# Experts of 24 token tiles computed by gathered rows, with exp buffers of two key tiles

## The reference

```python
qkv = x @ w_qkv; q, k, _ = split(qkv); k2 = own and previous window of 128 keys; v2 = k2
x0 = layernorm(x + (softmax(mask(q @ k2.T / 16)) @ v2) @ w_out + b_out)

q = k = rope(x0); v = x0          # in_proj with bias, 16 heads of width 16
attn = softmax(causal(q @ k.T / 4)) @ v   # over 2048 keys
x1 = layernorm(x0 + attn @ Wo.T + bo) * ln1_w + ln1_b
gates = softmax(x1 @ gate_w.T + gate_b)   # 8 experts
moe = sum over the 2 largest gates g_e: g_e * (x1 @ expert_w[e].T + expert_b[e])
x2 = layernorm(x1 + moe) * ln2_w + ln2_b
out = layernorm(x0 + x2)
```

## Time and profile before

| | us |
|---|---|
| median of 3 runs (1437.79 to 1442.79) | 1440.35 |
| profiled execution, device time | 1441.97 |
| its span from first to last instruction | 1440.2 |
| PE busy | 1388.6 |
| DVE busy | 1088.4 |
| ACT busy | 784.5 |
| POOL busy | 427.2 |
| last `pv` ends, from the span's start | about 1397.6 |

### The profile page before, as it was taken

How to read it: one execution, slowest core, us unless ns; L and a number is a source line. 1 busy time by engine, 2 the same in 40 slices (tenths; PEclk the granted TensorE clock), 3 DMA queues, 4 the chain that set the end, 5 groups by cost and what they waited for, 6 DMA issues and landing times.

```text
span 1440.2 us, 28031 instructions
## 1 busy us (share of the span) xinstructions
PE 1388.6 (96%) x9600; PEld 778.4 (54%) x9600; DVE 1088.4 (76%) x2736; ACT 784.5 (54%) x1707; POOL 427.2 (30%) x707
## 2 busy tenths in 40 slices
PE   8899999999999999999999999999999999999995
PEld 6767655554455545354656655555444355555542
DVE  3765877887797887778645897878778787888745
ACT  3235365555665555665654445554656567655651
POOL 4434522322232131112433543333121110111233
PEclk9999999999999999999999999999999999999997
DMA  3865422231211121121115232222120011111100
GB/s 116 196 175 130 126 57 61 57 80 27 64 47 47 40 59 46 28 57 27 48 54 148 80 90 68 57 58 64 31 60 21 23 26 26 34 32 43 25 23 12
DMA packets 161511, 88.56 MB, mean 61 GB/s; under 512 B 114166, under 2 KB 157998, under 8 KB 161115
## 3 DMA queue, kind: packets, MB, share of 16 engines
q1 hardware_dynamic: 161371, 86.78, 23.1%
HBM read 60.71 MB, written 25.43 MB: 60 GB/s over the span
## 4 chain that ended last, share of the span: by engine, by line
PE 47%; DVE 5%; issue 2%; ACT 2%; POOL 1%; DMA 1%; SPq 1%; POOLq 0%; DVEq 0%; ACTq 0%
PE bank L1533 11%; PE bank L1420 10%; PE bank L1397 8%; PE bank L1369 8%; DVE mxs L1061 2%; PE bank L1490 1%; ACT pbuf L974 1%; PE bank L1509 1%; PE bank L1373 1%; PE bank L1402 1%; PE bank L1519 1%; PE bank L1468 1%; PE bank L1451 1%; PE bank L1476 1%; PE bank L1426 0%
## 5 line engine op out<-in xcount | busy, mean ns | idle before, releaser
L1061 DVE TENSOR_REDUCE mxs<-bank 128x1 f32<-128x512 f32 (+3 forms) x1120 | 708.8, 667 | 145.7 <-PE bank L1369 75.3
L974 ACT ACTIVATE pbuf<-bank 128x512 f32<-128x512 f32 (+1 forms) x1112 | 589.0, 599 | 313.9 <-PE bank L1397 138.6
L1369 PE MATMUL bank<-ks,qs 96*128 96x512 bf16 (+3 forms) x1280 | 423.2, 349 | 5.8 <-DVE mxs L1061 3.5
L1397 PE MATMUL bank<-qs,ks 99*128 99x256 bf16 (+3 forms) x1536 | 421.8, 319 | 5.4 <-DVE mxs L1061 2.1
L1420 PE MATMUL bank<-pbuf,vcur 128*17 128x256 f32 (+3 forms) x3072 | 253.5, 469 | 0.3
L1397 PEld LDWEIGHTS bank<-qs,ks 99*128 99x128 bf16 x1536 | 142.6, 98 | 161.0 <-issue 41.1
L1533 PE MATMUL bank<-ew,x1T 128*128 128x512 f32 x464 | 222.4, 601 | 0.4 <-DVE mxs L1061 0.3
L1369 PEld LDWEIGHTS bank<-ks,qs 96*128 96x128 bf16 x1280 | 123.6, 99 | 128.9 <-issue 40.9
L1420 PEld LDWEIGHTS bank<-pbuf,vcur 128*17 128x17 f32 x3072 | 79.9, 97 | 147.4 <-issue 109.6
L1533 PEld LDWEIGHTS bank<-ew,x1T 128*128 128x128 f32 x464 | 82.0, 190 | 72.4 <-issue 60.8
L954 ACT ACTIVATE etmp<-bank,small 128x256 f32<-128x256 f32 x116 | 48.7, 471 | 80.2 <-PE bank L1533 80.2
(11 more groups left out here) (279 smaller groups left out, 1753.1 us busy)
## 6 DMA issues: line engine op xcount, KB each, us to landing
vcur<-v_scratch SPq DMA_DIRECT2D x92, 136.0 KB, 2.4
parts_scratch<-parts SPq DMA_DIRECT2D x29, 384.0 KB, 3.3
xw<-windows SPq DMA_DIRECT2D x29, 256.0 KB, 2.8
qs<-parts_scratch SPq DMA_DIRECT2D x32, 192.0 KB, 3.7
ks<-parts_scratch SPq DMA_DIRECT2D x28, 192.0 KB, 3.6
qs<-parts_scratch SPq DMA_DIRECT2D x32, 128.0 KB, 3.1
v_scratch<-vst SPq DMA_DIRECT2D x29, 136.0 KB, 2.3
x_scratch<-x SPq DMA_DIRECT2D x29, 128.0 KB, 1.7
```

The lines of the kernel that those rows point to most:

```text
L974: nc.scalar.activation(pbuf[:, u0:u0 + heads, nj * P - cols:nj * P], bk[:, 0:heads * cols].rearrange("p (h t) -> p h t", h=heads), ACT.Exp)\
L1061: v.reduce_max(mxs[:, j * HJ + h:j * HJ + h + heads, c], bk[:, 0:heads * cols].rearrange("p (h t) -> p h t", h=heads), AX_X)\
L1369: last = mm(bk[:, x * cols:(x + 1) * cols].rearrange("p (n t) -> p n t", t=P), qs6[0:KR, pos % QRING, head // HJ, j, head % HJ, :], ks5[0: ...
L1397: last = mm(bk[:, x * cols:(x + 1) * cols].rearrange("p (n t) -> p n t", t=P), ks5[0:KR + NPART, kslot, kb % GT, head, :], qs6[0:KR + NPAR ...
```

## The change

For the first 24 tiles (steps T < `SPARSE`) the dense expert steps are gone. The tiles are taken in three chunks of eight. For each tile x1 is stored in DRAM (`f_st`), as is x1 plus the weighted expert biases, and DVE and PE count which tokens chose which expert (`f_A` to `f_gt`). When a chunk is complete, DVE computes a table (`t_tab`): a place for each of the 2048 token and expert pairs, sorted by expert and padded so that each of 23 blocks of 128 rows has one expert. POOL scatters the tokens' numbers and gates to these places in 16 indirect transfers (`t_sc`), and SP loads the list (`t_id`). For each block SP loads the expert's weights (256 KB, `s_w`, the address read from the table), POOL gathers the rows of x1 (`s_g`), PE transposes (`s_T`) and multiplies by the one expert (`s_e`), ACT copies (`s_Tc`) and scales by the gates (`s_ec`), and SP stores the block (`s_st`). At last each tile's sum is loaded (`b_load`), and two indirect transfers of POOL add the two chosen rows to it (`b_g1`, `b_g2`, into two buffers by turns), behind which the norms run as steps `h_`, which are the `g_` steps on other buffers. The last eight tiles stay dense.

To make room in SBUF, `VRUN` goes from 4 to 2: `pbuf` is half as long, and PE does `pv` in runs of at most two key tiles. The whole order is computed anew, with the new steps' durations and, for the indirect transfers, times until they have landed (`INDIRECT`). The values 1300 and 1900 ns are what the change writes down for one indirect transfer on POOL.

```diff
-VRUN = 4
+VRUN = 2
...
+INDIRECT = {"s_g": 3600, "b_g1": 4000, "b_g2": 5000, "t_sc": 3600}
...
+SPARSE = 24
+CHUNK = 8
+CHUNKS = SPARSE // CHUNK
+BLOCKS = 2 * CHUNK + NE - 1
...
+    add("w_lists", 0, "POOL", 2500)
+    rows["w_lists", 0] = *rows["w_lists", 0][:2], 1.5, rows["w_lists", 0][3]
+    add("w_tri8", 0, "DVE", 100, ("w_lists", 0))
+    add("load_dummy", 0, "SP", 1500, ("w_lists", 0))
...
-        add("f_e0", T, "PE", 1720, ("d_x1Tc", T))
+        if T < SPARSE:
+            c, u = T // CHUNK, T // CHUNK * BLOCKS
...
+            add("f_A", T, "DVE", 100, ("f_ixf", T), ("t_tab", c - 1), ("w_tri8", 0))
+            add("f_A12", T, "DVE", 90, ("f_A", T), ("f_rk", T - 1), ("f_as", T - 1))
+            add("f_rk", T, "PE", 200, ("f_A12", T), ("f_as", T - 1), ("w_lists", 0))
+            add("f_as", T, "DVE", 90, ("f_rk", T), ("t_cnt", c - 1))
+            add("f_Rb", T, "DVE", 90, ("f_rk", T), ("t_tab", c - 1))
+            add("f_gt", T, "DVE", 90, ("f_top", T), ("t_sc", c - 1))
+            add("f_st", T, "SP", 900, ("f_acc0", T))
...
+            add("b_load", T, "SP", 450, ("f_st", T), ("h_aff2", T - 2), ("s_st", u + BLOCKS - 1))
+            add("b_g1", T, "POOL", 1900, ("t_tab", c), ("s_st", u + BLOCKS - 1), ("b_load", T))
+            add("b_g2", T, "POOL", 1900, ("b_g1", T))
+            back = c * CHUNK + CHUNK - 1 + 6 + 1.2 + (2.6 + 0.5 * i if c < CHUNKS - 1 else 1.3 + 0.25 * i)
...
+                add("t_cnt", c, "PE", 150, ("f_as", T))
+                add("t_tab", c, "DVE", 3500, ("t_cnt", c), ("f_Rb", T), ("f_gt", T), ("b_g2", c * CHUNK - 1), ("s_st", c * BLOCKS - 1), ("w_tri8", 0))
+                add("t_sc", c, "POOL", 2 * CHUNK * 1300, ("t_tab", c), ("load_dummy", 0))
+                add("t_id", c, "SP", 2500, ("t_sc", c), ("s_st", c * BLOCKS - 1))
...
+                    add("s_w", u + x, "SP", 900, ("t_tab", c), ("s_e", u + x - 2), ("w_o", 0))
+                    add("s_g", u + x, "POOL", 1300, ("t_id", c), ("f_st", last), ("s_T", u + x - 2))
+                    add("s_T", u + x, "PE", 215, ("s_g", u + x), ("s_Tc", u + x - 1))
+                    add("s_Tc", u + x, "ACT", 300, ("s_T", u + x), ("s_e", u + x - 2))
+                    add("s_e", u + x, "PE", 900, ("s_Tc", u + x), ("s_w", u + x))
+                    add("s_ec", u + x, "ACT", 300, ("s_e", u + x), ("s_st", u + x - 2), *[("h_store", c * CHUNK - 1)] * (x < 2))
+                    add("s_st", u + x, "SP", 900, ("s_ec", u + x))
...
+            add("h_load", T, "SP", 450, ("st0", tile), ("h_store", T - 2), ("s_st", u + BLOCKS - 1))
+            add("h_st", T, "DVE", 330, ("b_g2", T), ("h_norm3", T - 1))
+            add("h_mv", T, "DVE", 100, ("h_st", T))
+            add("h_rstd2", T, "POOL", 950, ("h_mv", T))
+            add("h_xb", T, "POOL", 700, ("h_load", T), ("h_rstd2", T))
+            add("h_norm2", T, "DVE", 370, ("h_mv", T))
+            add("h_aff2", T, "DVE", 370, ("h_norm2", T), ("h_xb", T))
+            add("h_zst", T, "DVE", 330, ("h_aff2", T))
+            add("h_zmv", T, "DVE", 100, ("h_zst", T))
+            add("h_rstd3", T, "POOL", 950, ("h_zmv", T))
+            add("h_norm3", T, "DVE", 320, ("h_rstd3", T))
+            add("h_store", T, "SP", 450, ("h_norm3", T))
...
+        wslot = [lodge(EC * E).rearrange("p (c d) -> p c d", c=EC) for _ in range(2)]
+        xslot, yslot = [lodge(E) for _ in range(2)], [lodge(E) for _ in range(2)]
+        xTslot = [lodge(EC * P).rearrange("p (c t) -> p c t", c=EC) for _ in range(2)]
...
+        accB, x0B = [lodge(E), yslot[0]], [lodge(E), yslot[1]]
...
+                elif name == "t_id":
+                    sp.wait_ge(ids_stored, 16 * 2 * CHUNK * (T + 1))
+                    if T:
+                        for x in range(T * BLOCKS - 2, T * BLOCKS):
+                            sp.wait_ge(xslot_loaded[x % 2], 16 * (x // 2 + 1))
+                    sp.dma_start(ids.rearrange("p (t o) -> p t o", o=2), id_dram[T].rearrange("(t p) o -> p t o", p=P),
+                                 allow_slow_non_contiguous=True).then_inc(ids_loaded, 16)
...
+                elif name == "s_w":
+                    u, t = T, T % BLOCKS
+                    sp.wait_ge(tab_step, TABS * (u // BLOCKS + 1))
+                    if u >= 2:
+                        sp.wait_ge(*fill("s_e", u - 2))
+                    col = sp.value_load(tab_w[0:1, t:t + 1], min_val=0, max_val=(NE - 1) * E)
+                    sp.dma_start(wslot[u % 2], exp_t[:, bass.ds(col, E)].rearrange("(c p) d -> p c d", p=P))\
+                        .then_inc(wslot_loaded[u % 2], 16)
...
+                elif name == "t_sc":
+                    pool.wait_ge(tab_step, TABS * (T + 1))
+                    if T == 0:
+                        pool.wait_ge(ids_loaded, 16 * CHUNKS)
+                    for x in range(2 * CHUNK):
+                        pool.indirect_dma_start(id_dram[T], bass.IndirectOffsetOnAxis(ap=placed[:, x:x + 1], axis=0),
+                                                own[:, x // 2, x % 2, :], None).then_inc(ids_stored, 16)
...
+                elif name == "s_g":
+                    u, t = T, T % BLOCKS
+                    pool.wait_ge(ids_loaded, 16 * (CHUNKS + u // BLOCKS + 1))
+                    pool.wait_ge(x1_stored, 16 * CHUNK * (u // BLOCKS + 1))
+                    if u >= 2:
+                        pool.wait_ge(*fill("s_T", u - 2))
+                    pool.indirect_dma_start(xslot[u % 2], None, x1_dram[u // BLOCKS], bass.IndirectOffsetOnAxis(
+                        ap=ids[:, 2 * t:2 * t + 1], axis=0)).then_inc(xslot_loaded[u % 2], 16)
...
+                elif name in ("b_g1", "b_g2"):
+                    k = int(name[3]) - 1
+                    if k == 0:
+                        pool.wait_ge(tab_step, TABS * (T // CHUNK + 1))
+                        pool.wait_ge(acc_loaded[T % 2], 16 * (T // 2 + 1))
+                        blocks_stored(pool, T)
+                    else:
+                        pool.wait_ge(gathered[T % 2], 32 * (T // 2) + 16)
+                    pool.indirect_dma_start(accB[T % 2], None, ys_dram[T // CHUNK], bass.IndirectOffsetOnAxis(
+                        ap=placed[:, 2 * (T % CHUNK) + k:2 * (T % CHUNK) + k + 1], axis=0), compute_op=ALU.add)\
+                        .then_inc(gathered[T % 2], 16)
...
+                elif name == "s_T":
+                    pe.wait_ge(xslot_loaded[T % 2], 16 * (T // 2 + 1))
+                    for c in range(EC):
+                        last = tr(bk[:, c * P:(c + 1) * P], xslot[T % 2][:, c * P:(c + 1) * P], idf[:, :])
+                    last.then_inc(filled[b], 1)
...
+                elif name == "s_e":
+                    pe.wait_ge(*drain("s_T", T))
+                    pe.wait_ge(wslot_loaded[T % 2], 16 * (T // 2 + 1))
+                    for c in range(EC):
+                        last = mm(bk[:, 0:E], xTslot[T % 2][:, c, :], wslot[T % 2][:, c, :], start=c == 0, stop=c == EC - 1)
+                    last.then_inc(filled[b], 1)
...
+                elif name == "s_ec":
+                    u = T
+                    act.wait_ge(*fill("s_e", u))
+                    if u >= 2:
+                        act.wait_ge(yslot_stored[u % 2], 16 * (u // 2))
+                    if u >= BLOCKS and u % BLOCKS < 2:
+                        act.wait_ge(back_out[1], 16 * (u // BLOCKS * CHUNK // 2))
...
```

423 lines of the change are left out of this document (344 added, 79 removed).

## The result

The changed kernel takes 1423.38 us (median of 4 runs, 1421.59 to 1425.19); the kernel before took 1440.31 beside it (1437.79 to 1442.79). The ratio is 0.9875, with a 95% interval from 0.9861 to 0.9889: 1.25% less, some 18 us. The forecast was 1397.

A forecast was written before the change was run, and what follows sets the result against it. PE's list of work was taken to bound the kernel up to the last pv, with an engine-to-engine tail behind. Work ending at 1323.2, new waits of 20 and a tail of 54 gave 1397 us, range 1364 to 1445.

The forecast's parts named there:

- What bounds the kernel: Whole kernel before: PE's list of work sets the time up to the last pv, then a 42.6 us engine-to-engine tail.
- PE's sum, -65.4: PE's work: dense steps -165.1, blocks +74.5, counting matmuls +5.0, shorter runs +20.2, together -65.4 us.
- The shorter runs: PE at pv: 192 runs instead of 100, each costing 0.22 us by itself, so 20.2 us more.
- New waits, 20: PE ahead of the last pv: 20 us of new waits, near the present rate once more.
- The range of 0 to 60: Bounds on new waits ahead of the last pv: lower 0, upper three chunks of 20 us.
- SP in front of the attention's loads: SP's queue: waits at t_id for all scatters of a chunk hold back vcur, parts and the next tiles' queries.
- POOL: POOL's work: 1.3 us per scatter or gather, 1.9 per adding gather, 243 us in all; busy some 620 us.
- The tail, 54: Behind the last pv: 54 us instead of 42.6, with 45 us in POOL's queue; bounds 43 to 65.
- Everything hides: Rival, whole kernel: no new waits and a tail of 43 to 45, 1367 us; chance 0.15 for 1350 to 1375.
- The ring of two binds: Rival at pv: 84 full-width rounds may each lose 0.5 us, +42, 1439 us; chance 0.18 for 1420 to 1445.
- Dear transfers: Rival: scatters on POOL delay SP at t_id and the attention's loads; 1459 us at 2.6 each; chance 0.17 above 1445.
- Faster: Forecast chance that the changed kernel beats the one before: 0.78, against same 0.05 and slower 0.17.

The follow-up runs named there:

- b_ring2: The kernel before with only VRUN cut from 4 to 2 and its order planned anew: 1459.5 us, ratio 1.0133.
- a_s16: The changed kernel with 16 tiles in gathered rows instead of 24, planned anew: 1438.15 us, ratio 0.9979.
- a_acc: The changed kernel with a sparse tile's sum written to idle buffer acc[0], so the projection no longer waits for its store, same order: 1417.55 us, ratio 0.9836.
- a_nosc: The changed kernel with two scatters in each chunk instead of sixteen, same order: 1416.46 us, ratio 0.9823.
- p_x1: a_plan with two buffers by turns for the tile stored for gathering (x1), same order: 1397.53 us, ratio 0.9695.
- a_nog: The changed kernel without POOL's adding gathers (experts' results left out), same order: 1414.45 us, ratio 0.9814.
- a_xb: a_plan with one addition of each of the last chunk's eight tiles moved from POOL to DVE: 1413.29 us, ratio 0.9796.
- a_nosplit: a_plan with the scatters again as one step of sixteen, planned anew: 1410.71 us, ratio 0.9786.
- p_jitter: a_plan with one planned cost (SP's issue of a block's weights) at 940 for 900 ns, giving another order: 1410.22 us, ratio 0.9802.
- a_spcost: The changed kernel with only the planned costs of SP's key and query issues corrected (0.62 us for 0.40, 0.45 by head group): 1460.53 us, ratio 1.0115.
- a_spcost_nosc: a_spcost with two scatters in a chunk instead of sixteen, same order: 1416.53 us, ratio 0.9827.
- a_plan: The changed kernel planned anew with the moved sum buffer, value loads first, scatters of two chunks split into twos, and measured costs: 1403.07 us, ratio 0.9742.
- p_x1_replan: p_x1 with the order planned anew for the freed wait, same work on every engine: 1413.91 us, ratio 0.9799.

## Why the forecast came out as it did

- **What bounds the kernel.** Right for the kernel before. The change turned some of that bound into waits: PE's idle time ahead of the last `pv` nearly doubled.
- **PE's sum, -65.4.** Busy time fell by 54.0. What the slower clock added has to be taken out first, by the same adding up as above over the whole span: 10.2 us before, 18.9 after. That leaves -62.7, so the sum was good to 2.7 us. The step length held: the table's 1365.99 to 1367.71 is 1.72 us again. Inside it two terms missed in opposite directions. The shorter runs cost PE 12.8 us of busy time, 13.9 at full clock, not 20.2 (b_ring2). The first two chunks together save 47.2, not 57.2 (a_s16 against b_ring2), and the third 29.4 (28.6 forecast); of the busy times alone, 1356.0 and 1334.6, one would read 21.4, the rest is clock.
- **New waits, 20: the step that failed.** The path lost 42.8 us (1366.0 less 1323.2): 29.0 of idle time, 10.7 of slower clock, for which the sum had no term ahead of the last `pv`, and 3 unassigned. I took "near the present rate once more", as if waits grew with the number of meetings. More than half of the new idle time lies in two stages instead (16.2 us in 5 and 6), behind a few places: a store that lands in 10 us (5.6 by a_acc), three bursts of scatters (7.5 by a_nosc, overlapping with the former), the ring (3.8 of idle time by b_ring2), and SP's queue behind the key and query burst, where PE waits 7 us, though no edit there brought a gain in the total that is clear of the noise. The rest of the 42.8 has no run of its own. In p_x1, where stores, queue and two of the bursts are mended, the last `pv` ends at 1335.7, which is 12.5 us by the same sum. The estimate fits that order, a lucky one; the kernel as built was not of that kind. The range of 0 to 60 held it.
- **SP in front of the attention's loads.** The rival was looked for at `t_id`, where SP waited 11.2 us at most. The late loads came where SP hardly waits but issues slower than planned, 0.62 us for the plan's 0.40. The earlier trace rows showed 0.37 for one transfer. SP's timeline of the kernel before had the burst too, and I did not read it:

```profile
765.90 0.56 SPq L777 DMA_DIRECT2D qs<-parts_scratch  x1
766.56 0.53 SPq L754 DMA_DIRECT2D ks<-parts_scratch  x1
767.20 0.56 SPq L777 DMA_DIRECT2D qs<-parts_scratch  x1
```

- **POOL.** Scatter 0.98 us busy and 1.27 from one to the next, gather 0.99, adding gather 1.64, so 1.3 and 1.9 were fair; busy 572 us against 620. The page's groups:

```profile
L1125 POOL DMA_INDIRECT gathering<-x_scratch,gathering x69 | 68.3, 990 | 182.1 <-PE bank L1928 158.5
L1136 POOL DMA_INDIRECT gathering<-ys_scratch,gathering x48 | 78.8, 1641 | 46.9 <-issue 18.1
L1117 POOL DMA_INDIRECT id_scratch<-gathering x48 | 46.8, 975 | 23.5 <-issue 13.7
```

  The gathers land in 3.4 and 4.0 us (medians), within my 2 to 4. The Trainium skill (DMA: Bandwidth & Descriptors, "Anatomy of one DMA") gives about 2.0 us fixed; the medians lie above that, and in the full stretch at 850 us plain transfers took 8 to 10. The Trainium skill's rule that such a transfer starves while VectorE holds the port pair (SBUF — State Buffer, "SBUF: two separate sides") found no sign here: 14 of the 16 scatters of the second chunk took 0.96 us, the others 0.98 and 1.12, with DVE at work beside them, mostly on row maxima read from PSUM.
- **The tail, 54.** It took 57.5, POOL busy 42.3 (45 forecast). POOL's share in it is shown by a_nog, 6.5 us; that POOL's row alone sets it is refuted by a_xb, a_nosplit and p_jitter. What sets it stays open. The clock fell there as before (mean 0.81, before 0.82).
- **The rivals.** *Everything hides*, at 1367, was reached by no run. That the best, p_x1 at 1397.5, equals the forecast confirms nothing: it is another kernel in a lucky order. *The ring of two binds* fell with b_ring2, and the median of ACT's waits for `pv` did not grow. (Its 84 rounds at full width are miscounted: of the 192 runs 72 have 512 columns throughout and 24 more in their first key tile; 0.5 us on each of the 96 would be 48 us, not 42.) *Dear transfers* named the steps that can cost and not the way: I looked for a scatter longer than 2.2 us and for SP waiting at the list. The scatters stayed short, and a_spcost still came out slower than the kernel before, because others stood still beside them.
- **The chances.** "Faster", at 0.78, came true. The time fell into the stretch from 1420 to 1445, which had 0.18 and was given to the ring. The ring was not the cause, so that this stretch held it is luck.

## What to carry to other kernels

Cost a stall by place, not by rate: look for the queue that will be longest at each point, reckon its pace from back-to-back rows of that very form, and list all that stands behind it, since moving one transfer only shows the next. Take the clock out of busy times before comparing them with a sum at full clock. With a planned order, compare several orders of the same work, and several executions of each, before crediting an edit with 5 to 15 us; here one trifling cost moved 8.6 us, and one order alone 6. Give each store its own buffer where landings can grow from 2.4 to 10 us, and where a kernel has bursts of small scatters, test it once without them.

## What was not expected of the hardware

- Beside sixteen scatters of 128 pairs of words, one every 1.27 us from POOL, PE's signals came up to several us late in one order, and ACT stood still for up to 8.6 us, PE, DVE and ACT together for up to 3.9, with no releaser that the profile names: 13 to 16 us a burst, 42 us in all (a_spcost against a_spcost_nosc). In the changed kernel's order the same bursts cost 7.5 us in all. The cause is open.
- Splitting a burst into steps of two with other work of POOL between them (a_plan, second chunk: from 818.2 to 870.9 us instead of 20 us) left no such standing still in its trace. But neither did a_plan's third burst nor a_nosplit's three, which are whole: the order decides, and that splitting helps against this is not shown.
- Executions of one order differ more in some orders: 1405.2 to 1419.9 us for p_x1_replan, 1394.0 to 1398.6 for p_x1, on the same chip. Why is not shown.
